# An attention and experts layer on one core: the gate is projected turned, head outputs are scaled by ScalarE after the last product and added by GpSimd

## The chip, the core and the metric

The kernel runs on one core of a Trainium2 chip. The metric is device time in microseconds (us) of one execution; lower is better. A core has TensorE (PE in the profile) for matmuls, VectorE (DVE), ScalarE (ACT) and GpSimd (POOL) for elementwise work, and the SP queue, which only issues DMAs here. TensorE writes to PSUM banks; GpSimd works in SBUF alone in this kernel.

## The reference

2048 tokens of width 256. 16 query heads and 4 key/value heads of 128; each group of 4 query heads shares a key/value head. Beside attention there are 8 experts, of which each token takes two. Cut to what matters:

```
xn = layernorm(x)
q, gate, k, v = split(xn @ w_qkv.T)
q, k = rope(layernorm(q)), rope(layernorm(k))
out  = softmax(causal(q @ k.T / sqrt(128))) @ v
out  = (out * sigmoid(gate)) @ w_o.T
x    = x + out + experts(xn)
```

## The kernel before

The outer loop runs over 4 groups g (one key/value head, 4 query heads), the inner one over 16 tiles t of 128 tokens. A tile (g, t) has t + 1 blocks of keys, so tiles grow towards the end of a group. A step of a tile has a name, and each engine has one queue in which the steps stand in an order written out by hand as a string of letters (`ORDERS`; `QUEUES` says which letter stands for which kind). Between engines, steps wait on semaphores alone. `BANKS` gives each step of TensorE that fills a PSUM bank one of five banks; `FREED_BY` names the step that lets it go. Two more banks hold turned scores (`pt_bank`), one holds the head outputs (`o_bank`).

f32 products are made of three passes (`three`, L1270): each operand is split into a high part, rounded to fp32r by ScalarE (`..._hi`), and the rest, by VectorE (`..._lo`). A turn is a transpose by TensorE.

The steps of a tile, by engine:

- `Q`, `KV`, `G` (TensorE, L1316): projections, tokens on the partitions. `G` fills one bank of 512 columns for the 4 heads: six passes.
- `q_take`, `kv_take` (ScalarE), `sumsq`, `same`, `rope_b` (VectorE), `swap`, `rstd` (GpSimd): layernorm and rope. `QT`, `KT` (TensorE) turn the result, `q_hi`, `q_lo` and so on split it.
- `scores` (TensorE), `max` (VectorE), `exp` (ScalarE, with row sums), `turn_probs` (TensorE), `p_hi`, `p_lo`, then `pv` (TensorE, L1358): the head outputs, with the head's dimension on the partitions and tokens on the columns, two heads (a half p) at a time, into `o_bank`.
- `inv` (VectorE, L1204): one over the row sums, `row_inv`.
- `tanh` (ScalarE, L873): sigmoid is (1 + tanh(gate / 2)) / 2; the half is in `w_o`. `gate_scale` (L905): four pieces of 128 columns, (tanh + 1) * `row_inv`, where tokens lie on the partitions, so that the row's scale is one number a partition. `GT` (TensorE, L1366): four turns bring the gate to the layout of the head outputs.
- `o_take` (ScalarE, L923): `o_bank` to `oT`, half by half; `pv` of the next tile waits for it. `og` (VectorE, L1210): `oT` times the turned gate. `og_hi` (L933), `og_lo` (L1215): its split.
- `OUT` (TensorE, L1374): 12 passes of 256 columns, summed over the 4 heads in one bank. `out_add` (VectorE, L1223): that bank is added to `acc`.

At the start `x` comes in five parts; `stats`, `x_rstd`, `norm` normalise a part (`xn`, L999), `XT`, `xT_hi`, `xT_lo` (L1004) turn and split it. `L`, `LT`, `route` choose the experts. The experts' steps (`XS`, `H`, `Y`, `fc_lo` ...) are strewn among the rest; GpSimd writes their rows with `scatter` and `y_place`. At the end `comb` (L1254) adds them to `acc`, and six stores write it out.

## Time and profile before

| | |
|---|---|
| median of 3 executions | 1523.54 us (1523.23 to 1524.11) |
| the profiled execution | 1523.42 us, of which the span from first to last instruction 1521.5 us |
| TensorE busy, matmuls | 1493.0 us, 98% of the span |
| VectorE, ScalarE, GpSimd busy | 1302.6, 1157.4, 369.3 us |
| granted clock of TensorE | 0.997 of 2.4 GHz |

Busy times are unions of an engine's instructions. A matmul's duration goes from its start to the end of its results, so neighbours overlap; what one more costs is the distance between starts.

### The profile page before, as it was taken

What the parts mean: (1) busy time and instruction counts of PE and PEld (TensorE: products, weight loads), DVE (VectorE), ACT (ScalarE), POOL (GpSimd) and SP (SyncE); (2) the same over time, 40 slices, a digit from 0 to 9 for tenths busy, and PEclk for the clock granted to TensorE, in tenths of its full rate; (3) what the DMA queues carried; (4) which work ended last, traced back from release to release, by engine and by line L of the source; (5) the groups of instructions that cost most, each with busy time, mean ns of one, the idle gap of its engine ahead of it and who ended that gap; (6) DMA issues with size and microseconds to landing.
All of it is one profiled execution on the core that took longest, in us unless ns stands there. A gap on an engine that the chain in (4) does not pass through costs nothing.

```text
span 1521.5 us, 29718 instructions
## 1 busy us (share of the span) xinstructions
PE 1493.0 (98%) x10589; PEld 1378.2 (91%) x10589; DVE 1302.6 (86%) x3037; ACT 1157.4 (76%) x3017; POOL 369.3 (24%) x502
## 2 busy tenths in 40 slices
PE   4999999999999999999999999999999999999998
PEld 3889999999999999999999999999999999999998
DVE  8999888888998888778799898877879988897888
ACT  3777777778888778777888777777788877767775
POOL 6644443330332211111032221111103231011010
PEclk9999999999999999999999999999999999999999
DMA  5510111002221021111122010111022111001014
GB/s 167 168 58 33 43 36 34 29 29 76 68 60 49 9 70 39 35 43 39 56 74 77 22 49 12 49 29 39 8 88 74 60 50 32 29 22 32 9 50 125
DMA packets 45124, 78.82 MB, mean 52 GB/s; under 512 B 4784, under 2 KB 30896, under 8 KB 44784
## 3 DMA queue, kind: packets, MB, share of 16 engines
q1 hardware_dynamic: 41232, 66.65, 14.3%
q0 software_dynamic: 3744, 10.26, 1.9%
q8 instruction: 84, 1.38, 0.4%
q14 instruction: 64, 0.52, 0.1%
HBM read 58.25 MB, written 24.72 MB: 55 GB/s over the span
## 4 chain that ended last, share of the span: by engine, by line
PE 83%; DVE 9%; issue 3%; ACT 3%; DMA 1%; POOL 0%; SPq 0%; DVEq 0%; ACTq 0%; POOLq 0%
PE bank L1270 43%; PE o_bank L1270 22%; PE pt_bank L1345 14%; DVE pT_lo L1194 2%; PE bank L1323 2%; PE bank L1366 1%; DVE neg_chunk_max L1180 1%; DVE bank L1177 1%; ACT probs L895 1%; DVE t_same L1144 1%; PE bank L1387 1%; ACT pT_hi L914 1%; DVE t_same L1140 0%; ACT gate L905 0%; DVE sumsq L1112 0%
## 5 line engine op out<-in xcount | busy, mean ns | idle before, releaser
L895 ACT ACTIVATE probs<-bank,neg_max 128x512 f32<-128x512 f32 (+3 forms) x640 | 397.0, 629 | 91.5 <-DVE neg_max L1187 51.3
L1194 DVE TENSOR_TENSOR pT_lo<-pt_bank,pT_hi 128x512 fp32r<-128x512 f32 (+1 forms) x576 | 368.6, 654 | 91.4 <-ACT pT_hi L914 88.4
L914 ACT ACTIVATE pT_hi<-pt_bank 128x512 fp32r<-128x512 f32 (+1 forms) x576 | 324.5, 578 | 136.5 <-PE pt_bank L1345 98.4
L1270 PE MATMUL o_bank<-pT_hi,v_hi 128*128 128x256 f32 x1088 | 328.3, 302 | 0.8 <-DVE pT_lo L1194 0.4
L1345 PE MATMUL pt_bank<-ident_rows,probs 128*128 128x128 f32 x2176 | 310.8, 273 | 0.7 <-DVE pT_lo L1194 0.2
L1270 PE MATMUL o_bank<-pT_hi,v_lo 128*128 128x256 f32 x1088 | 307.2, 282 | 0.0
L1270 PE MATMUL o_bank<-pT_lo,v_hi 128*128 128x256 f32 x1088 | 306.5, 282 | 0.0
L1180 DVE TENSOR_REDUCE neg_chunk_max<-bank 128x1 f32<-128x512 f32 (+1 forms) x384 | 242.7, 649 | 41.5 <-PE bank L1270 40.6
L1345 PEld LDWEIGHTS pt_bank<-ident_rows,probs 128*128 128x128 f32 x2176 | 252.5, 140 | 21.7 <-DVE pT_lo L1194 2.9
L1270 PE MATMUL bank<-kT_hi,qT_hi 128*128 128x512 f32 (+3 forms) x640 | 243.0, 380 | 0.2 <-ACT probs L895 0.2
L1270 PE MATMUL bank<-kT_lo,qT_hi 128*128 128x512 f32 (+3 forms) x640 | 231.1, 361 | 0.0
L1270 PE MATMUL bank<-kT_hi,qT_lo 128*128 128x512 f32 (+3 forms) x640 | 231.1, 361 | 0.0
L1270 PEld LDWEIGHTS o_bank<-pT_hi,v_hi 128*128 128x128 f32 x1088 | 206.4, 190 | 6.5 <-DVE pT_lo L1194 2.6
L1270 PEld LDWEIGHTS o_bank<-pT_lo,v_hi 128*128 128x128 f32 x1088 | 206.9, 190 | 3.1
L1270 PEld LDWEIGHTS o_bank<-pT_hi,v_lo 128*128 128x128 f32 x1088 | 206.1, 189 | 0.0
L756 POOL TENSOR_TENSOR t_swap<-qk_raw,made_tables 128x256 f32<-128x256 f32 (+1 forms) x160 | 86.8, 574 | 416.4 <-ACT t_same L864 416.1
L1270 PE MATMUL bank<-w_hi,xT_hi 128*128 128x512 f32 (+1 forms) x384 | 145.7, 379 | 8.7 <-DVE w_lo L1102 8.5
L1270 PE MATMUL bank<-w_hi,xT_lo 128*128 128x512 f32 (+1 forms) x384 | 137.4, 358 | 0.0
L1270 PE MATMUL bank<-w_lo,xT_hi 128*128 128x512 f32 (+1 forms) x384 | 137.3, 358 | 0.0
L1270 PEld LDWEIGHTS bank<-kT_hi,qT_lo 128*128 128x128 f32 x640 | 120.4, 188 | 17.2
L1270 PEld LDWEIGHTS bank<-kT_hi,qT_hi 128*128 128x128 f32 x640 | 121.1, 189 | 14.8 <-ACT probs L895 2.7
L895 ACT ACTIVATION_READ_ACCUMULATOR probs<-bank,neg_max 128x1 f32 x640 | 134.1, 210 | 0.0
(167 smaller groups left out, 2856.1 us busy)
## 6 DMA issues: line engine op xcount, KB each, us to landing
norm_rows<-kept_tables SPq DMA_DIRECT2D x24, 384.0 KB, 3.2
made_tables<-kept_tables SPq DMA_DIRECT2D x24, 384.0 KB, 3.3
kept_tables<-made_tables SPq DMA_DIRECT2D x16, 384.0 KB, 2.5
rows<-xs SPq DMA_DIRECT2D x23, 258.0 KB, 2.7
expert_raw<-in_w_fc SPq DMA_DIRECT2D x23, 256.0 KB, 3.1
expert_raw<-in_w_proj SPq DMA_DIRECT2D x23, 256.0 KB, 2.8
xs<-in_x_fill SPq DMA_DIRECT2D x11, 516.0 KB, 5.7
w_raw<-in_w_in SPq DMA_DIRECT2D x7, 640.0 KB, 4.3
```

The lines of the kernel that those rows point to most:

```text
L756: ins = pool.tensor_tensor(t_swap[:, heads, to], qk_raw[:, heads, of], rotary(g, t)[:, 1, i:i + 1, to].to_broadcast([P, count, 64]), ALU.mult)
L895: act.activation(probs[:, u, h % 2, first:first + width], bank("scores", g, t, h, c)[:, 0:width], ACT.Exp, bias=neg_max[:, u, h % 2:h % 2 ...
L914: act.activation(pT_hi[:, n % PT_RING, 0:width], pt_bank[n % 2][:, 0:width], ACT.Copy)\
L1144: ins = dve.scalar_tensor_tensor(rotated[:, h, :], t_same[:, h, :], rstd[:, h:h + 1], rotary(g, t)[:, 2, h // HG, :], ALU.mult, ALU.add)
L1177: ins = dve.tensor_tensor_reduce(scores, scores, mask[:, CHUNK - width:CHUNK], 1.0, least, ALU.add, ALU.min, to)
L1180: ins = dve.tensor_reduce(to, scores, AX.X, ALU.min)
L1194: dve.tensor_tensor(pT_lo[:, n % PT_RING, 0:width], pt_bank[n % 2][:, 0:width], pT_hi[:, n % PT_RING, 0:width].bitcast(F32), ALU.subtract) ...
L1270: ins = pe.matmul(out_ap, s, m, start=(start and done == 1), stop=(stop and done == last))
L1323: ins = pe.transpose(bank("QT", g, t)[:, h * P:(h + 1) * P], rotated[:, h, :], ident_f[:])
L1345: ins = pe.transpose(pt_bank[n % 2][:, (2 * jj + hh) * P:(2 * jj + hh + 1) * P], probs[:, p, hh, j * P:(j + 1) * P], ident_f[:])
L1366: ins = pe.transpose(bank("GT", g, t)[:, h * P:(h + 1) * P], gate[:, t % 2, h * D:(h + 1) * D], ident_f[:])
L1387: ins = pe.transpose(bank("XS", m)[:, (2 * c + k) * P:(2 * c + k + 1) * P], rows[:, k, c * P:(c + 1) * P], ident_f[:])
```

## The change

- `G` is projected turned: the weights of one head are the stationary operand and 256 tokens (two tiles, a pair) the moving one. A step `G` (g, pair, head) makes six passes of 256 columns. `tanh` writes it to `gateT` for each head. `GT` and `gate_scale` are gone.
- `og0` (VectorE) makes (tanh + 1) times `o_bank` in one instruction, half by half, straight from the bank to `oT`; `o_take` and `og` are gone. The row sums aren't in it yet. `og_hi` and `og_lo` form all four heads at once as before (the last tile in halves, as before).
- `OUT` no longer sums the heads: each half p fills a bank with the product of its two heads side by side. `o_scale` (ScalarE) multiplies each by its column of `row_inv`, one into `oT` (which is free by then), one into `o_rows` (in the place of `ogT_lo`). `out_add` (GpSimd) adds both to `acc`, one after the other. Only the last tile's is left to VectorE (`out_last`).
- `row_inv` has two buffers. `comb` and the stores wait for GpSimd's additions too. The orders of all engines and the banks are written anew.

```diff
--- before.py
+++ after.py
-FREED_BY = {"Q": "q_take", "KV": "v_lo", "G": "tanh", "QT": "q_lo", "KT": "k_lo", "GT": "og", "OUT": "out_add",
+FREED_BY = {"Q": "q_take", "KV": "v_lo", "G": "tanh", "QT": "q_lo", "KT": "k_lo", "OUT": "o_scale",
...
-    "dve": ("BCGHDHGGBGBBCCBJKDDJJCDDALLDDCPPKJPPJEQJQDEMDLLEIPPKJPPJMJNEQQLLOFPFFPPKPJJQQJNMNQLOLQFFPKPJJPPJMQNQNFLL"
+    "dve": ("BCGHDGBGCGHDDABBBCKCJDJEJDDDLLCOOOKJJEOPJMEDNPLLDINOOKJJOOJEFFFNPLLPKJOOOFMJFFNJNOPPFFFFLNMLPKJOPOOJNJPN"
...
-            add('pe G', ('G', g, t))
+            if t % 2 == 0:
+                for h in range(HG):
+                    add('pe G', ('G', g, t // 2, h))
+                    add('act gate', ('tanh', g, t // 2, h))
...
-            add('act gate', ('tanh', g, t))
             add('dve gate', ('inv', g, t))
-            add('act gate', ('gate_scale', g, t))
-            if (g, t) == LAST_TILE:
-                add('pe GT', ('GT', g, t))
-                for p in range(HG // 2):
-                    add('dve out', ('og', g, t, p))
+            for p in range(HG // 2):
+                add('dve og', ('og0', g, t, p))
+            for p in range(HG // 2):
+                if (g, t) == LAST_TILE:
                     add('act og', ('og_hi', g, t, p))
                     add('dve og', ('og_lo', g, t, p))
-                add('pe OUT', ('OUT', g, t))
-                add('pe OUT', ('OUT_rest',))
-                add('dve out', ('out_add', g, t))
-            else:
-                add('pe GT', ('GT', g, t))
-                add('dve out', ('og', g, t))
-                add('act og', ('og_hi', g, t))
-                add('dve og', ('og_lo', g, t))
-                add('pe OUT', ('OUT', g, t))
-                add('dve out', ('out_add', g, t))
+                elif p:
+                    add('act og', ('og_hi', g, t))
+                    add('dve og', ('og_lo', g, t))
+            for p in range(HG // 2):
+                add('pe OUT', ('OUT', g, t, p))
+                if (g, t) == LAST_TILE:
+                    add('dve out', ('out_last', g, t, p))
+                else:
+                    add('act out', ('o_scale', g, t, p))
+                    add('pool out', ('out_add', g, t, p))
...
-                add('act O', ('o_take', g, t, p))
...
-        gate = sb("gate", [P, 2, QW])
+        gateT = sb("gateT", [P, HG, 2 * P])
...
+        with nc.sbuf_tensor("o_rows", [P, HG // 2, C], F32) as o_rows:
+            pass
...
-            "GT": lambda g, t: (og_done, g * T + t + 1),
-            "OUT": lambda g, t: (acc_done, acc_number["out_add", g, t]),
+            "OUT": lambda g, t, p: (o_scaled, number["o_scale", g, t, p]),
...
+                elif kind == "out_add":
+                    g, t, p = a
+                    n = number[step]
+                    w.wait_ge(o_scaled, number["o_scale", g, t, p])
+                    if n > 1:
+                        w.wait_ge(pool_added, n - 1)
+                    pool.tensor_tensor(acc[:, t, :], acc[:, t, :], oT[:, 256 * p:256 * p + 256], ALU.add).then_inc(pool_step, 1)
+                    w.wait_ge(pool_step, n)
+                    pool.tensor_tensor(acc[:, t, :], acc[:, t, :], o_rows[:, p], ALU.add).then_inc(pool_added, 1)
...
-                    g, t = a
-                    n = g * T + t
-                    w.wait_ge(filled, fill["G", g, t])
-                    if n >= 2:
-                        w.wait_ge(filled, fill["GT", *tile_before(g, t, 2)])
-                    act.activation(gate[:, t % 2, :], bank("G", g, t)[:], ACT.Tanh, scale=0.5).then_inc(gate_done, 1)
+                    g, q, h = a
+                    n = g * T + 2 * q
+                    w.wait_ge(filled, fill["G", g, q, h])
+                    if n:
+                        w.wait_ge(o_gated, 2 * (n - 1) + h // 2 + 1)
+                    act.activation(gateT[:, h], bank("G", g, q, h)[:, 0:2 * P], ACT.Tanh, scale=0.5).then_inc(gate_done, 1)
...
-                elif kind == "gate_scale":
-                    g, t = a
+                elif kind == "o_scale":
+                    g, t, p = a
                     n = g * T + t
+                    w.wait_ge(filled, fill["OUT", g, t, p])
                     w.wait_ge(inv_done, n + 1)
-                    w.wait_ge(gate_done, n + 1)
-                    for h in range(HG):
-                        gh, inv = gate[:, t % 2, h * D:(h + 1) * D], row_inv[:, h:h + 1]
-                        ins = act.activation(gh, gh, ACT.Identity, bias=inv, scale=inv)
-                    ins.then_inc(gated, 1)
+                    for i, rows_to in enumerate((oT[:, 256 * p:256 * p + 256], o_rows[:, p])):
+                        h = 2 * p + i
+                        ins = act.activation(rows_to, bank("OUT", g, t, p)[:, i * C:(i + 1) * C], ACT.Copy,
+                                             scale=row_inv[:, t % 2, h:h + 1])
+                    ins.then_inc(o_scaled, 1)
...
-                elif kind == "o_take":
-                    g, t, p = a
-                    n = g * T + t
-                    w.wait_ge(pv_done, number["pv", g, t, p, (t + 2) // 2 - 1])
-                    if n:
-                        w.wait_ge(og_lo_done, n)
-                    act.activation(oT[:, 256 * p:256 * p + 256], o_bank[:, 256 * p:256 * p + 256], ACT.Copy)\
-                        .then_inc(o_copied, 1)
                 elif kind == "og_hi":
-                    g, t, p = a if len(a) == 3 else (*a, None)
-                    n = g * T + t
-                    cols = slice(0, QW) if p is None else slice(256 * p, 256 * p + 256)
-                    if n:
-                        w.wait_ge(filled, fill["OUT", *tile_before(g, t)])
-                    w.wait_ge(og_done, n + 1 + (p or 0))
+                    g, t = a[0:2]
+                    p = a[2] if (g, t) == LAST_TILE else 1
+                    cols = slice(256 * p, 256 * p + 256) if (g, t) == LAST_TILE else slice(0, QW)
+                    w.wait_ge(o_gated, 2 * (g * T + t) + p + 1)
                     act.activation(ogT_hi[:, cols], oT[:, cols], ACT.Copy).then_inc(og_hi_done, 1)
...
-                elif kind == "og":
-                    g, t, p = a if len(a) == 3 else (*a, None)
-                    cols = slice(0, QW) if p is None else slice(256 * p, 256 * p + 256)
-                    w.wait_ge(filled, fill["GT", g, t])
-                    w.wait_ge(o_copied, 2 * (g * T + t) + (2 if p is None else p + 1))
-                    dve.tensor_tensor(oT[:, cols], bank("GT", g, t)[:, cols], oT[:, cols], ALU.mult).then_inc(og_done, 1)
+                    if i >= 2:
+                        w.wait_ge(o_scaled, number["o_scale", *tile_before(g, t, 2), 1])
+                    dve.reciprocal(row_inv[:, t % 2], row_sum[:]).then_inc(inv_done, 1)
+                elif kind == "og0":
+                    g, t, p = a
+                    n, q = g * T + t, t // 2
+                    cols, tokens = slice(256 * p, 256 * p + 256), slice((t % 2) * P, (t % 2 + 1) * P)
+                    w.wait_ge(pv_done, number["pv", g, t, p, (t + 2) // 2 - 1])
+                    w.wait_ge(gate_done, number["tanh", g, q, 2 * p + 1])
+                    if n:
+                        w.wait_ge(pool_added, number["out_add", *tile_before(g, t), p])
+                    dve.scalar_tensor_tensor(oT[:, cols].rearrange("p (h q) -> p h q", h=2), gateT[:, 2 * p:2 * p + 2, tokens], 1.0,
+                                             o_bank[:, cols].rearrange("p (h q) -> p h q", h=2), ALU.add, ALU.mult).then_inc(o_gated, 1)
                 elif kind == "og_lo":
-                    g, t, p = a if len(a) == 3 else (*a, None)
-                    cols = slice(0, QW) if p is None else slice(256 * p, 256 * p + 256)
-                    w.wait_ge(og_hi_done, g * T + t + 1 + (p or 0))
+                    g, t = a[0:2]
+                    cols = slice(256 * a[2], 256 * a[2] + 256) if (g, t) == LAST_TILE else slice(0, QW)
+                    w.wait_ge(og_hi_done, number["og_hi", *a])
                     dve.tensor_tensor(ogT_lo[:, cols], oT[:, cols], ogT_hi[:, cols].bitcast(F32), ALU.subtract)\
                         .then_inc(og_lo_done, 1)
-                elif kind == "out_add":
-                    g, t = a
-                    w.wait_ge(filled, fill["OUT", g, t])
-                    if (g, t) == LAST_TILE:
-                        w.wait_ge(last_out, 1)
+                elif kind == "out_last":
+                    g, t, p = a
+                    w.wait_ge(filled, fill["OUT", g, t, p])
+                    w.wait_ge(inv_done, g * T + t + 1)
+                    w.wait_ge(pool_added, number["out_add", g - 1, t, 1])
                     w.wait_ge(acc_done, acc_before[step])
-                    dve.tensor_tensor(acc[:, t, :], bank("OUT", g, t)[:, 0:C], acc[:, t, :], ALU.add)\
-                        .then_inc(acc_done, 1)
+                    for i in range(2):
+                        h = 2 * p + i
+                        dve.scalar_tensor_tensor(acc[:, t, :], bank("OUT", g, t, p)[:, i * C:(i + 1) * C], row_inv[:, t % 2, h:h + 1],
+                                                 acc[:, t, :], ALU.mult, ALU.add).then_inc(acc_done, 1)
+                        w.wait_ge(acc_done, acc_number[step] - 1 + i)
...
+                    w.wait_ge(pool_added, number["out_add", G - 2 if t >= LATE_COMB else G - 1, t, 1])
...
+                elif kind == "G":
+                    g, q, h = a
+                    tokens = slice(2 * q * P, 2 * (q + 1) * P)
+                    cols = slice(QW + 2 * D + h * D, QW + 2 * D + (h + 1) * D)
+                    w.wait_ge(wg_lo_done, 2 * g + 2)
+                    w.wait_ge(xT_lo_done, 2 * part_of(2 * q + 1) + 1)
+                    three(bank("G", g, q, h)[:, 0:2 * P], [(w_hi[:, c, cols], w_lo[:, c, cols]) for c in range(CT)],
+                          [(xT_hi[:, c, tokens], xT_lo[:, c, tokens]) for c in range(CT)]).then_inc(filled, 1)
...
-                        w.wait_ge(o_copied, 2 * (g * T + t) + p)
+                        w.wait_ge(o_gated, 2 * (g * T + t) + p)
...
-                elif kind == "GT":
-                    g, t = a
-                    w.wait_ge(gated, g * T + t + 1)
-                    for h in range(HG):
-                        ins = pe.transpose(bank("GT", g, t)[:, h * P:(h + 1) * P],
-                                           gate[:, t % 2, h * D:(h + 1) * D], ident_f[:])
+                elif kind == "OUT":
+                    g, t, p = a
+                    w.wait_ge(og_lo_done, number["og_lo", g, t, p] if (g, t) == LAST_TILE else number["og_lo", g, t])
+                    w.wait_ge(wo_lo_done, g + 1)
+                    for i in range(2):
+                        h = 2 * p + i
+                        rows_of = slice(h * P, (h + 1) * P)
+                        ins = three(bank("OUT", g, t, p)[:, i * C:(i + 1) * C], [(ogT_hi[:, rows_of], ogT_lo[:, rows_of])],
+                                    [(wo_hi[:, h, :], wo_lo[:, h, :])])
                     ins.then_inc(filled, 1)
-                elif kind == "OUT":
-                    g, t = a
-                    w.wait_ge(og_lo_done, g * T + t + 1)
-                    w.wait_ge(wo_lo_done, g + 1)
-                    heads = range(HG) if (g, t) != LAST_TILE else range(HG // 2)
-                    three(bank("OUT", g, t)[:, 0:C], [(ogT_hi[:, h * P:(h + 1) * P], ogT_lo[:, h * P:(h + 1) * P]) for h in heads],
-                          [(wo_hi[:, h, :], wo_lo[:, h, :]) for h in heads], stop=(g, t) != LAST_TILE).then_inc(filled, 1)
-                elif kind == "OUT_rest":
-                    g, t = LAST_TILE
-                    w.wait_ge(og_lo_done, g * T + t + 2)
-                    heads = range(HG // 2, HG)
-                    three(bank("OUT", g, t)[:, 0:C], [(ogT_hi[:, h * P:(h + 1) * P], ogT_lo[:, h * P:(h + 1) * P]) for h in heads],
-                          [(wo_hi[:, h, :], wo_lo[:, h, :]) for h in heads], start=False).then_inc(last_out, 1)
```

## Rows read from the trace of the kernel before

**Rows 1.** The page: busy times, and the engines' shares of the chain that ended last.

```profile
PE 1493.0 (98%) x10589; PEld 1378.2 (91%) x10589; DVE 1302.6 (86%) x3037; ACT 1157.4 (76%) x3017; POOL 369.3 (24%) x502
...
PE 83%; DVE 9%; issue 3%; ACT 3%; DMA 1%; POOL 0%; SPq 0%; DVEq 0%; ACTq 0%; POOLq 0%
```

**Rows 2.** Three stretches: length, busy of PE, PEld, DVE, ACT, POOL, clock, DMA.

```profile
0.00:60.00 60.00, 38.88 (x223) 30.82 (x223) 51.80 (x149) 32.90 (x88) 38.98 (x60) 0.94 0.52 172
60.00:1480.00 1420.00, 1416.62 (x10086) 1312.73 (x10086) 1214.18 (x2814) 1100.47 (x2875) 330.29 (x443) 1.00 0.15 45
1480.00:1521.50 41.50, 37.49 (x283) 34.68 (x281) 36.63 (x76) 24.04 (x56) 0.00 (x0) 0.98 0.37 115
```

**Rows 3.** The table of waits, TensorE: what for, us in total, times, longest.

```profile
PE bank L1270 <- DVE w_lo L1102: 8.5, 1, 8.5
PE bank L1284 <- DVE xn L999: 5.8, 2, 5.2
PE bank L1323 <- DVE t_same L1144: 4.2, 2, 3.3
PE bank L1284 <- DVE v_lo L1133: 3.5, 2, 3.3
```

**Rows 4.** The chain of waits, 1495 us to the end: start, length, what.

```profile
1496.61 1.39 PE bank L1270 x6
1498.00 0.44 PE pt_bank L1345 x4
1498.44 0.73 PE o_bank L1270 x6
```

**Rows 5.** The chain of waits, 1508 us to the end.

```profile
1515.98 0.39 ACT oT L923
...
1517.38 0.44 DVE ogT_lo L1215
...
1517.86 0.99 PE bank L1270 x6
...
1518.97 0.42 DVE acc L1223
```

**Rows 6.** TensorE's groups of instructions, shapes apart.

```profile
L1366 PE MATMUL bank<-ident_rows,gate 128*128 128x128 f32 x256 | 38.4, 272 | 0.0
```

**Rows 7.** ScalarE's groups of instructions, shapes apart.

```profile
L905 ACT ACTIVATE gate<-gate,row_inv 128x128 f32<-128x128 f32 x256 | 105.6, 492 | 3.8 <-DVE row_inv L1204 2.8
...
L895 ACT ACTIVATE probs<-bank,neg_max 128x256 f32<-128x256 f32 x112 | 53.9, 483 | 6.2 <-DVE neg_max L1177 6.1
L923 ACT ACTIVATE oT<-o_bank 128x256 f32<-128x256 f32 x128 | 50.0, 391 | 22.5 <-PE o_bank L1270 19.8 <-DVE ogT_lo L1215 2.4
L933 ACT ACTIVATE ogT_hi<-oT 128x512 fp32r<-128x512 f32 x63 | 40.0, 635 | 16.2 <-DVE oT L1210 16.0
...
L873 ACT ACTIVATE gate<-bank 128x512 f32<-128x512 f32 x64 | 38.3, 598 | 8.9 <-PE bank L1270 8.6
```

**Rows 8.** VectorE's groups of instructions, shapes apart.

```profile
L1210 DVE TENSOR_TENSOR oT<-bank,oT 128x512 f32<-128x512 f32 x63 | 43.0, 683 | 3.8 <-PE bank L1366 3.6
```

**Rows 9.** Lines by themselves: count, shortest, median and longest in ns.

```profile
L1223 DVE TENSOR_TENSOR acc<-bank,acc x64: 394/415/426, 65.2 to 1519.0; 128x256 f32<-128x256 f32 x64
...
L1254 DVE SCALAR_TENSOR_TENSOR acc<-y_rows,p,acc x32: 472/484/486, 1474.5 to 1518.2; 128x256 f32<-128x256 f32 x32
...
L745 POOL TENSOR_TENSOR made_tables<-made_tables,t_swap x16: 729/738/1803, 20.3 to 306.7; 128x256 f32<-128x256 f32 x16
...
L1215 DVE TENSOR_TENSOR ogT_lo<-oT,ogT_hi x65: 412/682/1257, 56.2 to 1517.4; 128x512 fp32r<-128x512 f32 x63, 128x256 fp32r<-128x256 f32 x2
```

**Rows 10.** The timeline's start, VectorE and TensorE.

```profile
17.34 4.53 DVE L999 TENSOR_SCALAR xn<-acc,probs 128x256 f32<-128x256 f32 x7
...
24.48 1.01 DVE L1004 TENSOR_TENSOR xT_lo<-bank,xT_hi 128x384 fp32r<-128x384 f32 x2
...
28.81 1.09 PE L1323 MATMUL bank<-ident_rows,t_same 128*128 128x128 f32 x4 [3.29 <-DVE t_same L1144]
```

202 lines of the change are left out of this document (103 added, 99 removed).

## The prediction, made before the changed kernel was run

> **What bounds the kernel now.** I read the page's busy times first: TensorE is busy 98% of a span of 1521.5 us, VectorE 86%, ScalarE 76%, GpSimd 24% [rows 1]. A busy matmul row is a modelled time, so I asked next where TensorE stands still. The stretches answer that: in 0 to 60 us it idles 21.1 us, in 60 to 1480 us only 3.4 of 1420, in the last 41.5 us 4.0 [rows 2]. The table of TensorE's waits says that 22.0 us of it are four waits of the start: for a split weight, for xn, for the rotated heads, for a bank [rows 3]. So from 60 us on TensorE's own instructions set the time, nearly one for one, and the other engines matter only where they come to hold it up. In the chain of waits near the end the pieces of TensorE follow each other without a gap, and give prices by difference of starts: four f32 turns of 128 columns 0.44 us, six passes of 256 columns 0.72 us, six passes of 512 columns 1.39 us [rows 4]. These are the prices to use; the mean of one turn, 272 ns [rows 6], is latency and overlaps its neighbours.
>
> **TensorE's part of the change.** Removed: `GT`, 64 steps of four turns [rows 6]: 64 x 0.44 = 28.2 us. Changed: `G`. Before, 64 steps of six passes of 512 columns: 64 x 1.39 = 89.0 us. After, for each pair of tiles and each head six passes of 256 columns: 32 x 4 x 0.72 = 92.2 us, so 3.2 us more. `OUT` keeps its 12 passes of 256 columns a tile, in two banks instead of one: nothing, and `scores`, `turn_probs`, `pv`, `Q`, `KV` and the experts keep theirs. Sum: -28.2 + 3.2 = -25.0 us. Bounds: a turn has as many columns as half a pass of 256, so it can't well cost less than 0.06 us, which leaves a gain of 12 us; the 0.44 for four is measured between steps of `pv` and others, where `GT` stood too, so I hold to it. If the smaller passes cost exactly half of the large ones (64 x 1.39 for all), the gain is 28.
>
> **ScalarE's part.** Removed: 256 pieces of the gate's scaling 105.6 us, 128 copies of `o_bank` 50.0 us, 64 tanh of 512 columns 38.3 us [rows 7], together 193.9. Added: 128 tanh of 256 columns, at the price of the 256-column copy, 0.39 us: 50 us; and 252 `o_scale` pieces of 256 columns out of a bank, with a scale read from memory. No row shows that one. The copy without such an operand, 0.39 us, is below it; the exp of 256 columns, which reads one such operand, 0.48 us; the gate's scaling reads two and takes 105.6/256 = 0.41 us for 128 columns, so for 256 at most 0.52. I take 0.48: 121 us, with 98 to 131 as bounds. Net -23 us (-46 to -13): ScalarE is no nearer to being the bound.
>
> **VectorE's part.** Removed: 63 `og` of 512 columns 43.0 us and two of 256, 0.8; 63 `out_add` at 0.42, 26 us [rows 8]. Added: 128 `og0` of 256 columns (one scalar_tensor_tensor). The nearest rows are the 256-column addition out of a bank, 0.42, and the `comb` form, 0.48 [rows 8, 9]: 54 to 61 us, I take 0.45, 58 us; and `out_last`, 4 x 0.48 = 1.9 against one 0.42. Net about -11 us. Per microsecond of TensorE's work it stays as loaded as it was (1292 of 1468 against 1303 of 1493), and in 60 to 1480 it still has some 200 us of idle time [rows 2].
>
> **GpSimd's part.** 126 `out_add` steps, each two additions of 128x256 that depend on each other. The row for just this form, `made_tables`, has a median of 738 ns, at worst 1803 [rows 9]. 252 x 0.74 = 186 us: from 369 to 555 us, 36% of the span. This is hidden as work; it counts only as a delay.
>
> **The waits.** (a) *The head outputs.* `pv` of the next tile waited for `o_take`, now for `og0`, which waits for `tanh` and for GpSimd's `out_add` of the tile before, since `oT` is also where scaled rows go. In VectorE's queue, behind a waiting `og0`, stand `p_lo` and `max`, and TensorE waits for those. From an end of `OUT` (half 0) the way is two `o_scale` 0.96, two additions 1.5 to 1.6, then `og0` 0.45: 3.0 us, if GpSimd is free; a `swap`, `rstd` or `y_place` ahead adds 1 to 2. I laid TensorE's step prices along the new order string: from the end of `OUT` (g, t, 0) to the first `pv` that needs `og0` of the next tile freed, there are 7.8 us or more for every tile. So TensorE's direct wait is covered with 4 us to spare. ScalarE's queue gets two waits of the kind too: `tanh` of the next pair waits for `og0` of the tile before (one buffer of `gateT` where `gate` had two), `o_scale` for `OUT`; behind them stand `exp` and `p_hi`. GpSimd's `out_add` waits for `o_scale`, and behind it stand `swap`, `rstd` and `y_place`, of which `QT` needs the first two, some 2 tiles ahead. All three are covered while `og0` is in time. (b) *`og_hi` and `og_lo`.* They now come after `og0` of half 1: 0.45 + 0.64 + 0.68 = 1.8 us to `OUT` [rows 7, 9]. The same count over the string gives 2.0 us or more between the last `pv` of a tile and `OUT`, but for one place: at tile (1, 0) only one `turn_probs` of 0.44 stands between. There I expect a wait of 1.4 us. (c) *Banks.* 64 more fills of `G`, 64 more of `OUT`, 64 fewer of `GT`: 64 more in all over the same five banks, but `OUT` is let go after 0.96 us. I cost it at nothing: 1239 fills instead of 1175 over five banks in 1500 us are one for each bank in 6.1 instead of 6.4 us, and most are held for a pass of TensorE and one or two short instructions. If that cover is gone, it is rival C. (d) *The start.* VectorE's new order puts `norm` 3, `xT_lo` 1 and 2 and `wr_lo` ahead of `sumsq` (0, 0). That is four norms (2.6 us by the 4.53 for seven, 1.7 at the 0.42 of another 256-column instruction), 1.0 us, and a short one for which I put 0.4: `QT` (0, 0) falls 3.1 to 4.0 us later than 28.8 [rows 9, 10]. But `L` 0 (six passes of 512 columns, 1.39), `LT` 0 (four small turns, 0.3) and an `XT` of 0.44 have moved into that gap. So +1.0 to +1.9; I take 1.5. (e) *The end.* After the last `pv`: before, `o_take` 0.39, `og`, `og_hi`, `og_lo` 0.44, `OUT` 0.99 and `out_add` 0.42, from 1515.98 to 1519.39 [rows 5]. After: no copy, but `og_lo` twice and two dependent `out_last` pieces of 0.48 for each half in place of one of 0.42: -0.4 + 0.4 + 0.5 = +0.5 us. The stores keep their form. SP's queue has as many steps as before.
>
> **The sum.** The profiled execution took 1523.4 us against a median of 1523.5, so nothing is to be corrected. 1523.4 - 25.0 + 1.5 + 1.4 + 0.5 = 1501.8 us.
>
> **Weighed against this: the shared port.** [Rows 9] show an `og_lo` of 1257 ns beside a median of 682, and a GpSimd addition of 1803 beside 738: either engine is now and then held about one instruction of the other. The Trainium skill, page "SBUF — State Buffer", section "SBUF: two separate sides", states an exclusive lock between a GpSimd operation and a VectorE one with two SBUF inputs, in which the loser fully blocks; the long durations agree with it. In rows: GpSimd's additions cover 186 of 1502 us, 12%. About 620 VectorE instructions read two SBUF operands (`same`, `rope_b`, `og_lo`, the expert splits). 12% of them are 76, each held 0.37 on average: 28 us more on VectorE. Were each on TensorE's path, the time would be 1530; with VectorE's idle time as cover, I give half of it in the rival and nothing in the forecast.
>
> **Rivals.** *A, slower: the loop through GpSimd.* In 32 of the 63 tiles, by the count above, less than 3.0 us of TensorE's work lies between the end of `OUT` (half 0) and the end of the next tile's last `pv` of that half; there `og0` waits in VectorE's queue with `p_lo` behind it. For it: the chain that ended last lies for 9% of the span on VectorE and for 3% on ScalarE [rows 1], so in places TensorE already runs just behind them. Against it: the two banks and three buffers of turned scores that lie between, and that TensorE lost 3.4 us in 1420 with a queue like this. It decides from 22/32 = 0.7 us of TensorE's time for each such tile on; at 1.2 us the time is 1501.8 + 38 = 1540. *B, the shared port*, as above: 1501.8 + 14 = 1516, or 1508 at a quarter. *C, most of the gain goes into waits at banks and `og0`*, 0.35 us in each of the 63 tiles: 1501.8 + 22 = 1524, no change. For it: more hand-overs between engines; against: ScalarE and VectorE each have less to do. *D, more gain*: passes at half price, no stall at the start or at (1, 0): 1523.4 - 28 = 1495.5.
>
> **How the numbers follow.** Forecast (1497 to 1507) 0.58, B 0.16, D 0.10, C 0.06, A 0.10. About 0.2% (3 us) is what a measurement can tell from no change. Faster: forecast, B and D, 0.84. Same: C, 0.06. Slower: A, 0.10. Leaving out A, C and the edges of B and D gives 1494 to 1514.
>
> **What would show it.** Right: TensorE's busy time near 1468, no wait of TensorE over 2 us after 60 us but near tile (1, 0), GpSimd near 555 us, `o_scale` 0.45 to 0.52, idle time of 60 to 1480 under 8 us. Wrong: TensorE's idle time between 60 and 1480 us above 15 us, with `p_lo` or `scores` as what ends it and `og0` waiting for GpSimd (A); `og_lo` and `rope_b` clearly longer in the mean (B); busy time of TensorE fallen by less than 20 us (the price of a turn).

## The result: 1.1% slower, where 1.4% faster was forecast

| | before | after | forecast |
|---|---|---|---|
| median | 1523.8 us | 1541.2 us (1540.2 to 1541.9) | 1501.8, range 1494 to 1514 |
| ratio | | 1.0113, 95% interval 1.0102 to 1.0125 | 0.986 |
| span of the profiled execution | 1521.5 | 1540.0 | |

One of the four executions of the kernel before took 1631.4 us, over 7% above the other three, and the ratio leaves it out.

The page of the changed kernel, busy times and the engines' shares of the chain that ended last (before: [rows 1]):

```profile
PE 1487.3 (97%) x10717; PEld 1380.4 (90%) x10717; DVE 1321.8 (86%) x3040; ACT 1122.9 (73%) x2949; POOL 561.7 (36%) x754
...
PE 73%; DVE 13%; issue 7%; POOL 4%; ACT 2%; DMA 1%; SPq 0%; DVEq 0%; POOLq 0%; ACTq 0%
```

TensorE is busy 6 us less, not 25; VectorE is busy 19 us more, not 11 less; its share of the chain is 13% where it was 9%. GpSimd is near where it was expected (561.7 against 555). The three stretches (before: [rows 2]):

```profile
0.00:60.00 60.00, 38.43 (x202) 30.60 (x203) 49.87 (x140) 27.86 (x70) 35.68 (x59) 0.89 0.49 159
60.00:1480.00 1420.00, 1393.59 (x10110) 1298.58 (x10110) 1219.87 (x2795) 1058.54 (x2792) 519.80 (x687) 1.00 0.14 45
```

TensorE's idle time between 60 and 1480 us is 26.4 us where it was 3.4: the prediction had named 15 as the sign that it is wrong. The table of TensorE's waits (before: [rows 3]):

```profile
PE bank L1347 <- DVE t_same L1147: 15.4, 14, 2.5
PE bank L1300 <- DVE xn L1002: 13.6, 2, 8.4
PE bank L1313 <- ACT logit_rows L826: 3.0, 2, 2.3
PE pt_bank L1369 <- ACT probs L909: 2.7, 4, 0.9
PE bank L1286 <- DVE ogT_lo L1227: 2.7, 3, 1.3
PE pt_bank L1369 <- DVE pT_lo L1197: 2.6, 7, 0.8
```

At the top stands a wait that was 4.2 us in two places and is now 15.4 in 14: `QT` for `rope_b`. VectorE's and GpSimd's groups say why (out<-in, count, busy us, mean ns, idle before):

```profile
L1147 DVE SCALAR_TENSOR_TENSOR t_same<-t_same,rstd,made_tables 128x128 f32<-128x128 f32 x200 | 68.1, 406 | 1.5
L1143 DVE TENSOR_TENSOR t_same<-t_same,t_swap 128x640 f32<-128x640 f32 x64 | 56.5, 883 | 1.1
L1221 DVE SCALAR_TENSOR_TENSOR oT<-gateT,o_bank 128x256 f32<-128x256 f32 x128 | 52.9, 414 | 21.3 <-PE o_bank L1286 11.6 <-POOL acc L788 8.0 <-ACT gateT L887 1.0
L1227 DVE TENSOR_TENSOR ogT_lo<-oT,ogT_hi 128x512 fp32r<-128x512 f32 x63 | 46.0, 730 | 3.3 <-ACT ogT_hi L936 3.3
...
L1147 DVE SCALAR_TENSOR_TENSOR t_same<-t_same,rstd,norm_rows 128x128 f32<-128x128 f32 x120 | 43.1, 423 | 0.8
```

```profile
L788 POOL TENSOR_TENSOR acc<-acc,o_rows 128x256 f32<-128x256 f32 x126 | 101.0, 802 | 9.9
L786 POOL TENSOR_TENSOR acc<-acc,oT 128x256 f32<-128x256 f32 x126 | 95.2, 756 | 336.3 <-ACT o_rows L919 333.2
```

`rope_b` has not been changed, but its 128-column pieces last 406 and 423 ns in the mean. In the kernel before the same form stands at

```profile
L1144 DVE SCALAR_TENSOR_TENSOR t_same<-t_same,rstd,made_tables 128x128 f32<-128x128 f32 x200 | 56.1, 347 | 1.4
```

A place in the timeline of the changed kernel shows it at work (start, length; other rows between them left out):

```profile
1183.65 0.82 DVE L1143 TENSOR_TENSOR t_same<-t_same,t_swap 128x640 f32<-128x640 f32 x1
...
1184.06 0.28 PE L1286 MATMUL o_bank<-pT_lo,v_hi 128*128 128x256 f32 x1
...
1184.18 0.28 PE L1286 MATMUL o_bank<-pT_hi,v_lo 128*128 128x256 f32 x1
1184.20 0.85 POOL L786 TENSOR_TENSOR acc<-acc,oT 128x256 f32<-128x256 f32 x1 [0.74 <-ACT o_rows L919]
...
1184.51 2.28 DVE L1147 SCALAR_TENSOR_TENSOR t_same<-t_same,rstd,norm_rows 128x128 f32<-128x128 f32 x5
1185.13 0.72 POOL L788 TENSOR_TENSOR acc<-acc,o_rows 128x256 f32<-128x256 f32 x1
...
1186.94 1.08 PE L1347 MATMUL bank<-ident_rows,t_same 128*128 128x128 f32 x4 [2.48 <-DVE t_same L1147]
...
1187.89 0.77 PE L1286 MATMUL bank<-w_hi,xT_hi 128*128 128x512 f32 x1
```

The two additions fall on `rope_b`, its five pieces take 2.28 us, and TensorE stands for 2.48. The five pieces by themselves (shortest, median and longest in ns; then the first one alone):

```profile
L1147 DVE SCALAR_TENSOR_TENSOR t_same<-t_same,rstd,norm_rows x5: 337/339/875, 1184.5 to 1186.5; 128x128 f32<-128x128 f32 x5
...
1184.51 0.70 DVE L1147 SCALAR_TENSOR_TENSOR t_same<-t_same,rstd,norm_rows 128x128 f32<-128x128 f32 x1
```

Three of them are as short as ever; the two that meet an addition take 0.70 and 0.88 us, and end at 1185.20 and 1186.00, each 0.15 us after an addition has ended (1185.05 and 1185.85). So it is in the whole trace: of the 320 pieces 57 overlap an addition, in 24 of the 64 `rope_b`, and last 719 ns in the mean; the other 263 last 346. 42 of the 57 last over 500 ns, and every one of these ends 0.146 to 0.161 us after an addition. A piece isn't slowed by an addition, it stands until the addition is over. Why do they meet? In GpSimd's queue `out_add` often stands behind `rstd`, and `rope_b` comes some time after `rstd` too. It isn't `rstd` that starts it, though: here `rstd` was done at 1183.47, VectorE still had `same` to do, and over the whole run the first piece starts 2.4 us (median) after the end of its `rstd`. (The two passes above also show what the page's busy time hides: a row lasts 0.28 us, the next starts 0.12 us later. A wait of up to 0.16 us between two such passes leaves no gap in the busy time.)

### The profile page after: what moved, and what is told of

Same layout as the page of the kernel before. It is cut to its first block, busy times and chain, and to the rows that moved or that the text cites. A ratio compares the mean times of both kernels' runs of the same rounds, so it can differ in the third digit from the quotient of the medians.

```text
span 1540.0 us, 30508 instructions
## 1 busy us (share of the span) xinstructions
PE 1487.3 (97%) x10717; PEld 1380.4 (90%) x10717; DVE 1321.8 (86%) x3040; ACT 1122.9 (73%) x2949; POOL 561.7 (36%) x754
## 4 chain that ended last, share of the span: by engine, by line
PE 73%; DVE 13%; issue 7%; POOL 4%; ACT 2%; DMA 1%; SPq 0%; DVEq 0%; POOLq 0%; ACTq 0%
PE bank L1286 38%; PE o_bank L1286 20%; PE pt_bank L1369 12%; DVE t_same L1147 3%; PE bank L1347 2%; DVE pT_lo L1197 2%; POOL t_swap L761 1%; DVE neg_chunk_max L1183 1%; DVE bank L1180 1%; DVE t_same L1143 1%; POOL rstd L770 1%; DMA w_raw<-in_w_in 1%; DVE sumsq L1115 1%; POOL acc L788 1%; DVE t_same L1131 1%
## 5 line engine op out<-in xcount | busy, mean ns | idle before, releaser
L1369 PE MATMUL pt_bank<-ident_rows,probs 128*128 128x128 f32 x2176 | 316.6, 274 | 5.9 <-ACT probs L909 2.7
L786 POOL TENSOR_TENSOR acc<-acc,oT 128x256 f32<-128x256 f32 x126 | 95.2, 756 | 336.3 <-ACT o_rows L919 333.2
L795 POOL DMA_INDIRECT y_of<-rows,row_to x46 | 47.6, 1035 | 224.7 <-issue 184.8
L1286 PEld LDWEIGHTS bank<-kT_lo,qT_hi 128*128 128x128 f32 x640 | 121.7, 190 | 8.4
```

The source lines that it names most:

```text
L786: pool.tensor_tensor(acc[:, t, :], acc[:, t, :], oT[:, 256 * p:256 * p + 256], ALU.add).then_inc(pool_step, 1)
L795: pool.indirect_dma_start(y_of, bass.IndirectOffsetOnAxis(row_to[:, k:k + 1], 0), rows[:, k, 0:C], None)\
L1286: ins = pe.matmul(out_ap, s, m, start=(start and done == 1), stop=(stop and done == last))
L1369: ins = pe.transpose(pt_bank[n % 2][:, (2 * jj + hh) * P:(2 * jj + hh + 1) * P], probs[:, p, hh, j * P:(j + 1) * P], ident_f[:])
```

## The experiments

Eighteen runs, each beside the kernel before on the same chip. "After" stands for the changed kernel. Where a run is compared with one of another group, it is by the ratios.

**1. The additions, taken away or replaced.** Theory P: GpSimd's additions hold VectorE's instructions with two operands in SBUF. Theory Q: the way through GpSimd's queue is too long. Theory O: the new order of the steps costs the time, whatever GpSimd does.

```diff
-                    pool.tensor_tensor(acc[:, t, :], acc[:, t, :], oT[:, 256 * p:256 * p + 256], ALU.add).then_inc(pool_step, 1)
-                    w.wait_ge(pool_step, n)
-                    pool.tensor_tensor(acc[:, t, :], acc[:, t, :], o_rows[:, p], ALU.add).then_inc(pool_added, 1)
+                    # a_no_adds: nothing; og0 waits for o_scale instead
+                    # a_fills_for_adds: five chained memsets of 128x176, one of a column, the same waits
```

(The expectation speaks of six memsets; it was five of 176 columns and one of a single column.)

> The changed kernel with GpSimd's 252 additions left out (the attention part doesn't reach the sum; og0 waits for o_scale instead). Changed kernel 1541, before 1524. Theory P (the additions hold VectorE's two-operand instructions at the shared port): VectorE's busy time falls from 1322 to about 1292 and rope_b's pieces from 406-423 ns back to 347; the time falls by most of the 43 us that TensorE lost, to 1500 to 1510. Theory Q (the additions delay swap and rstd in GpSimd's queue, and with them QT): the same fall, so this run doesn't tell P from Q. Theory O (the new order of the steps itself, above all at the start of the run and at the small tiles of each group, costs the time whatever GpSimd does): stays at 1530 or above, idle time of TensorE in 60 to 1480 us stays near 25 us.

> The changed kernel, each pair of additions replaced by six memsets of a spare tile, which read nothing, with the same waits and about the same length (some 1.6 us a step; the attention part doesn't reach the sum). Theory P (shared port): most of the loss goes, 1505 to 1515, rope_b's pieces near 347 ns. Theory Q (queue of GpSimd and the wait of og0): stays within 5 us of 1541. Theory O: stays near 1541 too, but then a_no_adds does as well.

Measured: without additions 1523.1 us, ratio 0.9987 (0.9977 to 0.9997); with memsets 1520.3, 0.9969 (0.9956 to 0.9981). In the second GpSimd is busy 529.9 us (561.7 with additions, 365.0 with nothing), and `og0` waits for it 9.0 us, as before, yet its page and its table of TensorE's waits say:

```profile
PE 1476.2 (97%) x10717; PEld 1375.6 (91%) x10717; DVE 1291.4 (85%) x3040; ACT 1121.6 (74%) x2949; POOL 529.9 (35%) x1258
```

```profile
PE bank L1352 <- DVE t_same L1152: 4.1, 4, 1.7
```

VectorE is at the forecast 1292 us, and `rope_b`'s pieces are at 347 and 348 ns. So of the distance between 1541 and the forecast, 0.0144 of the time, 22 us, is what the additions do to VectorE (19 by the run without any), and GpSimd's queue costs nothing that can be seen: Q's 1541 is out. The other 18 us are not theirs. P's own times, 1500 to 1510 and 1505 to 1515, were missed for that reason, and so were O's 1530 or more: each theory had been given the whole loss. That the run without additions is slower than the one with memsets is in its trace in part: TensorE stands 3.7 us for `oT` at 293 us, and runs slower behind it (granted clock 0.66 from 290 to 300 us); the times of its ten executions lie between 1519.9 and 1525.0.

**2. The additions alone, in the kernel before.** Behind each `rstd` of groups 1 to 3, GpSimd works on 256 columns that are free there; nothing waits for it.

```diff
                     pool.tensor_tensor(rstd[:], variance[:], minus_half[:], ALU.pow).then_inc(rstd_done, 1)
+                    if g:
+                        # b_adds_held_in_before only: w.wait_ge(rotated_done, n + 1)
+                        for i in range(4):
+                            w.wait_ge(spare_step, 4 * (n - T) + i + 1)
+                            pool.tensor_tensor(spare_rows, spare_rows, spare_rows, ALU.add).then_inc(spare_step, 1)
+                            # b_one_operand: pool.tensor_scalar(spare_rows, spare_rows, 1.0, None, ALU.mult)
+                            # b_fills: ten memsets of 128x176 in the place of the four
```

> The kernel before with four dependent additions of 128x256 on a spare tile in GpSimd's queue behind each rstd of groups 1 to 3 (192 in all, 142 us of GpSimd; nothing waits for them but GpSimd's queue). Theory P: they meet rope_b head on; its pieces go to 450 ns or more, VectorE +25 us, the time +10 to +25 (1534 to 1549). Theory Q: swap of the next tile comes up to 3.1 us later only where it was within that of the rstd before; small, +0 to +8. Theory O: no change, 1524.

> The same as b_adds_in_before with ten memsets of a spare tile (about the same 3.2 us) in place of the four additions. Theory P: no change, 1524 to 1527. Theory Q: the same time as b_adds_in_before. Theory O: no change.

> The kernel before with the same 192 extra dependent GpSimd additions of 128x256 as in the run that took 1562.8 us, but each four wait until VectorE has finished the rope_b of their own tile. Theory P: an addition that meets no rope_b costs little; rope_b's pieces at 350 ns, TensorE's waits for QT near 4 us, and 1524 to 1534. Rival P2 (each addition costs VectorE the same wherever it falls): 1550 to 1565.

> The kernel before with, in the place of the 192 extra additions (two reads of memory each), 192 multiplications of 128x256 by a constant, which read one operand. Theory P by reading as such: any instruction of GpSimd that reads memory holds VectorE's two-operand instructions for its length; so the loss goes with GpSimd's added busy time: if one takes 0.4 to 0.5 us instead of 0.74, the loss is 20 to 26 us, 1544 to 1550. Rival P3 (only instructions with two reads hold VectorE): 1520 to 1526, as with memsets. Rival P4 (one that reads a single operand holds it all the same and takes as long): near 1563.

| | ratio | to before | rope_b's pieces, two forms | VectorE busy (before 1302.6) | GpSimd's added work |
|---|---|---|---|---|---|
| 192 additions behind rstd | 1.0252 (1.0235 to 1.0269) | +37.8 us | 408, 495 ns | 1344.4 us | 141 us, 736 ns each |
| the same, held until rope_b is done | 1.0052 (1.0035 to 1.0069) | +7.9 | 348, 348 | 1311.8 | 122 us, 634 ns |
| 192 multiplications with one operand | 1.0040 (1.0026 to 1.0054) | +5.9 | 357, 369 | 1311.5 | 177 us, 921 ns |
| 480 memsets | 0.9984 (0.9975 to 0.9994) | -2.6 | 347, 347 | 1302.7 | 117 us, 245 ns |

(The first form, with `made_tables`, also counts the 80 pieces of group 0, where nothing was added; the second stands in groups 1 to 3 alone.)

GpSimd's groups in the held and the one-operand run:

```profile
L774 POOL TENSOR_TENSOR angles<-angles 128x256 f32<-128x256 f32 x192 | 121.7, 634 | 190.7 <-DVE t_same L1153 179.4
```

```profile
L773 POOL TENSOR_SCALAR angles<-angles 128x256 f32<-128x256 f32 x192 | 176.9, 921 | 12.0
```

Additions that nobody needs cost 38 us, and 30 of them go when only their moment changes. So theory P holds: what counts is which instructions of VectorE they meet, and `rope_b` is the dear one. The rival by which each addition costs the same wherever it falls is out (it had said 1550 to 1565). P's size was wrong: it had expected 25 us on VectorE and 10 to 25 in the time, and got 42 and 38. In the trace 87 pieces of `rope_b` meet an addition and last 697 ns, the other 233 last 345. And it isn't reading as such: 177 us of one-operand work at the same place cost 6, where P by reading had said 20 to 26. There 185 pieces meet a multiplication and last 373 ns, at most 495. The time grows by 0.9 of what VectorE's busy time grows by, with the additions held as without; of the 38 us 14 are waits of `QT` that the table shows (18.0 us against 4.2). That the rest comes by `QT` too is not shown. The 2.6 us that the memsets seem to gain are unexplained.

**3. Can the changed kernel be mended so?** Hold each addition until `rope_b` of the tile ahead is done (where VectorE doesn't need it first); or give the first scaled pieces memory of their own in groups 1 to 3, so that not `og0` but only the later `og_lo` waits for GpSimd; or both.

```diff
+                    # held: the last rstd ahead of this step in GpSimd's queue
+                    w.wait_ge(rotated_done, len(ropes))
                     if n > 1:
                         w.wait_ge(pool_added, n - 1)
+                    # apart: angles and norm_rows[:, 3] in the place of oT; og_lo, not og0, waits for pool_added
```

> The changed kernel, complete; in 110 of the 126 out_add steps GpSimd now waits, ahead of its first addition, until VectorE has finished the rope_b whose rstd stands last before it in GpSimd's queue (in the other 16 VectorE needs the addition first). The additions read as much memory as before and keep their place in every queue; they only no longer meet rope_b. Theory P (the additions hold VectorE's rope instructions, QT comes late): rope_b's 128-column pieces fall from 406 ns to near 350, TensorE's waits for QT from 15.4 us in 14 to 4 to 8 us, and the time from 1541 to 1525 to 1532; not to the 1520 of the fills, since the additions now meet og_lo and the splits instead. Rival P2 (what is held is VectorE's work in all, wherever the additions fall): pieces of rope_b at 350, but other two-operand lines longer by as much, and 1537 to 1543. Rival Q2 (a later addition holds og0, and what stands behind it): 1545 or more, with TensorE waiting for oT or pT_lo.

> The changed kernel, complete, but in groups 1 to 3 o_scale puts its first piece of each half into memory of its own (256 columns that held the angles, 256 that held a norm row) instead of oT. So og0 of the next tile no longer waits for GpSimd's additions; og_lo does, over a microsecond later, since it writes where the second pieces lie. The additions keep their number and place. Theory P alone (the additions cost by the instructions of VectorE that they meet, the way through GpSimd costs little while nothing is held): 1538 to 1542, rope_b's pieces still 400 to 410 ns. Rival A of the prediction (the way through GpSimd is itself dear): 1525 to 1533.

> The kernel of the run before (first pieces in memory of their own), complete, with each addition also held until rope_b of the tile ahead is done, where VectorE doesn't need it earlier. If holding the additions failed before only because og0 waited for them (33.7 us of VectorE's time), the two together give what each alone could not: rope_b's pieces near 350 ns, VectorE's wait of og0 for GpSimd under 5 us, and 1520 to 1527, near the run with fills. Rival (the port takes its toll from og_lo, same and the splits just as well): 1532 to 1542.

Measured: held 1.0130 (1.0113 to 1.0147), apart 1.0122 (1.0105 to 1.0138), both 1.0071 (1.0055 to 1.0088). After itself: 1.0113. The held run, `og0`'s group on VectorE:

```profile
L1226 DVE SCALAR_TENSOR_TENSOR oT<-gateT,o_bank 128x256 f32<-128x256 f32 x128 | 53.3, 416 | 45.7 <-POOL acc L793 33.7 <-PE o_bank L1291 10.1 <-ACT gateT L892 1.0
```

`rope_b` is back at 348 ns and VectorE at 1298 us, but `og0` now waits 33.7 us for GpSimd instead of 8.0, with `p_lo` and `max` behind it: the loss has moved, not gone. That is between rival P2's 1537 to 1543 and Q2's 1545 or more, and TensorE's 5.4 us of waits for `oT` are Q2's sign; P's 1525 to 1532 is missed. So the change has tied the additions from both sides. Early they meet `rope_b`, late they hold `og0`. With memory apart the second tie is loosened, and the two together give back 6 us that neither gives alone (apart alone: as the theory had it, with `rope_b` at 405 and 424 ns). My 1520 to 1527 was still too good, and the rival's 1532 to 1542 has the time, though not the mechanism: `og_lo` takes 721 ns there and 730 in after, `same` 727 and 740: `rope_b` was as short as expected (347 ns), but TensorE stood 4.6 us at one place near 515 us, where ScalarE and VectorE both waited for loads (an expert's weights, a rotation table); why these came late there was not followed up. It ends 10.7 us above before.

**4. The rest of the distance: start and gate.** Theory O: the new order of the start. VectorE does `rope_b` (0, 0) ahead of norm 3 and route 0, ScalarE the copy of logits 3 ahead of two exps, TensorE `QT`, `KT` (0, 0), `Q` (0, 1) ahead of `XT` 5 and 6 (first try; the second, shown below, leaves xT_lo 3 ahead of `same` (0, 0) and does xT_lo 4 too ahead of norm 3, since they free the banks).

```diff
+MOVES = (    # engine, step, the step that it now stands ahead of
+    ('dve', ('norm', 3), ('xT_lo', 5)),
+    ('dve', ('route', 0), ('xT_lo', 5)),
...
+    ('act', ('q_hi', 0, 0), ('xT_hi', 5)),
+    ('act', ('logit_copy', 3), ('exp', 0, 1, 2, 0)),
+    ('pe', ('QT', 0, 0), ('XT', 5)),
+    ('pe', ('KT', 0, 0), ('XT', 5)),
+    ('pe', ('Q', 0, 1), ('XT', 5)),
+)
```

> The changed kernel, complete, with a few steps of its first 55 us in another order: VectorE does the first tile's same and rope_b before norm 3, xT_lo 3 and route 0, q_lo and k_lo before xT_lo 5; ScalarE does q_hi and k_hi before xT_hi 5 and logit_copy 3 before two exps; TensorE does QT, KT and Q (0, 1) before XT 5 and 6. Banks stay with their steps. Theory O (a part of the loss is the new order of the start, with the slower clock that its idle time brings): QT (0, 0) at 27.5 to 28.5 us instead of 30.7, no wait of 2.4 us for logit_rows, and 4 to 6 us less in all: 1535 to 1537. Rival O2 (what is gained at the start is lost again, because the same chain of rope, exp and turned scores sets the pace of the first tiles): less than 1.5 us, 1540 to 1541.

> The changed kernel, complete, with the start in another order, mended after the first try, in which KT (0, 0) waited for a bank that xT_lo 4 frees: VectorE does rope_b (0, 0), xT_lo 3 and 4 before norm 3, route 0 and q_lo, k_lo; the rest as in the first try. Theory O: QT (0, 0) at 28 to 28.5 us, KT within 1.5 us behind it, no wait for logit_rows above 1 us, and 3 to 5 us less than 1541. Rival O2 (the first tiles' chain of rope, max, exp and turned scores sets the pace, and TensorE has too little other work until tile (0, 3)): 1539.5 to 1542.

> The changed kernel with tanh writing gateT as before but og0 reading a constant in its place, so that tanh, which has one buffer for a pair of tiles, no longer waits for og0 of the pair before (10.2 us of ScalarE's waits, in 6). The gate is left out of the result. If the single buffer of the gate is part of the loss (ScalarE stands still with exp and p_hi behind): 2 to 6 us less, 1535 to 1539, above all in the small tiles. If those waits are covered: 1540 to 1542.

Measured: 1.0146 (1.0129 to 1.0163), 1.0141 (1.0124 to 1.0158), gate 1.0131 (1.0114 to 1.0147). All three miss their times. In the first try `QT` (0, 0) starts at 28.9 instead of 30.7 us, but `KT` waits 2.3 us for its bank; in the second xT_lo 3 stands waiting in VectorE's queue with `same` behind it, and `QT` starts at 30.2. Neither order is a fair test of a better start; they show only that it isn't mended by moving a step or two. Without the wait for the single buffer of the gate nothing is gained (two executions took 1543.9 us, two 1547.3): ScalarE's 10.2 us of waiting there are covered.

**5. What is TensorE's work worth?** The prediction rests on the step that it is worth its length. Theory R: in the small tiles of each group VectorE is as full as TensorE, so that what TensorE is spared there turns into waiting. So: take work from TensorE alone, in the old order (one turn of the gate for four, 63 times; `og` multiplies all heads by that one in an instruction of the same size), from VectorE alone (`same` of one query head for four), and from ScalarE (one piece of the gate's scaling for four).

```diff
-                    for h in range(HG):
+                    for h in range(HG if (g, t) == LAST_TILE else 1):
                         ins = pe.transpose(bank("GT", g, t)[:, h * P:(h + 1) * P],
...
-                    dve.tensor_tensor(t_same[:, 0:HG, :], qk_raw[:, 0:HG, :],
+                    dve.tensor_tensor(t_same[:, 0:heads, :], qk_raw[:, 0:heads, :],
```

> The kernel before, its order unchanged, with one turn of the gate instead of four in 63 of its 64 GT steps; og multiplies all four heads by that one turned head, in one instruction of the same size, so VectorE's, ScalarE's and GpSimd's work stays. The other three heads' gates are left out of the result. Removed: 63 x 3 turns, 20.8 us of TensorE by the 0.44 for four. If TensorE's work is worth its length wherever it lies, as the prediction took it: 1502 to 1505. Theory R (in the small tiles of each group VectorE is as full as TensorE, 28 to 29 us of 30, so what TensorE is spared there turns into waiting): a gain of 12 to 16 us only, 1508 to 1512, with new waits of TensorE in the first eight tiles of the groups. Rival R2 (order and hand-overs bind everywhere): under 8 us of gain.

> The same shortening of same in the kernel before, for comparison: 27 us less of VectorE, TensorE's work unchanged, the same part left out of the result. TensorE waits 3.4 us there in 60 to 1480 us, so there is little to win: 1520 to 1523 by either theory. More than 5 us of gain would say that VectorE held TensorE back already, out of sight of the waits.

> The run with fills in the place of the additions, and in it the wide piece of same (VectorE, 0.70 us) multiplies one query head instead of four in 63 tiles: 0.42 us less of VectorE in each tile, 27 us in all, with no wait changed and TensorE's work unchanged. The rotation of three query heads is left out of the result. Theory R (VectorE's load in the small tiles holds back a part of TensorE's saving): 1512 to 1517 against 1520.3. Rival (what is left is the chain of hand-overs, or the start): 1519 to 1521.

> The kernel before with both cuts at once: one turn of the gate instead of four (20.8 us of TensorE, alone worth 6.7) and the short same (27 us of VectorE, alone worth 3.8); the same parts are left out of the result. If TensorE and VectorE bind together (each one's saving is held back by the other), the two give clearly more than their sum of 10.5: 15 to 22 us less, 1502 to 1509. If they are independent: 1512 to 1515. If a third thing binds (ScalarE, or the chain from one step to the next): 1512 to 1516 as well, and the next run tells.

> The kernel before with one turn of the gate instead of four and one piece of the gate's scaling on ScalarE instead of four in 63 tiles (77 us less of ScalarE, and the scaled gate 1.2 us earlier); only the first head's gate counts in the result. If ScalarE's queue is what holds TensorE's saving back: 1503 to 1511. If not: 1515 to 1518, as with the quarter turns alone.

> All three cuts in the kernel before: turns, same, and the gate's scaling. If all engines are tied to each other through the fixed order, this gives the 20.8 us of TensorE nearly whole: 1499 to 1504. If what holds the saving back is not the load of VectorE or ScalarE but the length of the chain for one block (scores, max, exp, turns, splits, pv), then no more than the run with the turns and same together.

| | taken away | ratio | to before |
|---|---|---|---|
| turns | TensorE 20.8 us by price | 0.9955 (0.9938 to 0.9972) | -6.7 us |
| same | VectorE 25 by its rows, 19 of busy time | 0.9975 (0.9964 to 0.9985) | -3.9 |
| turns and same | both | 0.9939 (0.9923 to 0.9956) | -9.3 |
| turns and gate's scaling | TensorE 20.8, ScalarE 64 of busy time | 0.9935 (0.9918 to 0.9951) | -10.0 |
| all three | all | 0.9912 (0.9895 to 0.9928) | -13.4 |
| memsets for additions, in the new order (experiment 1) | | 0.9969 (0.9956 to 0.9981) | -4.7 |
| the same and short same | VectorE 25 by its rows, 22 of busy time | 0.9931 (0.9914 to 0.9948) | -10.8 |

(The expectations put the work taken away at 27 and 77 us.) Of 20.8 us taken from TensorE, 6.7 arrive (4.3 to 9.4 by the interval). That refutes the one-for-one step for this kernel in its old order; what an order written anew for the lighter work would give was not run. The page of that run still looks as before:

```profile
PE 1484.0 (98%) x10400; PEld 1358.8 (90%) x10400; DVE 1302.3 (86%) x3037; ACT 1154.9 (76%) x3017; POOL 366.5 (24%) x502
```

```profile
60.00:1480.00 1420.00, 1412.33 (x9946) 1297.78 (x9946) 1219.02 (x2826) 1101.50 (x2884) 329.30 (x443) 1.00 0.14 45
```

98% busy, 7.7 us idle from 60 to 1480: 4.3 more than before, where 14 are missing. The rest are the waits too short to be seen whole in the busy time. (The Trainium skill, page "Perfetto Trace Analysis", in the note at its head, calls matmul busy time a bad metric, since matmuls are pipelined, and names MFU, the share of peak arithmetic, and the busy share of weight loads instead. That matmul busy time is a bad metric agrees with these rows; the share of weight loads would not have helped: PEld is 91% before and 90% here. MFU was not worked out.) To see them I gave each of TensorE's steps its price by difference of starts ([rows 4]; a 512-column pass 0.23, a turn 0.11) and took the sum along the order from the time between the first and the last step ("fills" are the memsets of experiment 1):

| waits of TensorE over its steps' prices, us | in all | 0 to 100 | 100 to 400 | 400 to 500 | 500 to 800 | 800 to 900 | 900 to 1100 | 1100 to 1300 | later |
|---|---|---|---|---|---|---|---|---|---|
| before | 38.5 | 24.2 | 1.5 | 1.2 | 3.1 | 1.8 | 0.5 | 3.0 | 3.1 |
| turns taken away | 53.7 | 26.0 | 3.8 | 2.6 | 5.9 | 3.3 | 2.1 | 5.5 | 4.5 |
| after, with fills | 61.5 | 31.0 | 7.8 | 7.1 | 4.5 | 2.6 | 1.3 | 5.0 | 2.2 |
| after | 81.7 | 32.4 | 6.2 | 8.9 | 4.2 | 8.3 | 3.4 | 13.5 | 4.8 |

The sums hang on the prices: with slightly other ones (0.2317, 0.1198, 0.1747 and 0.1093 us for passes of 512, 256 and 384 columns and a turn) they are 36.5, 51.7, 58.8 and 79.1, so 2 to 3 us lower each, and their differences within 0.7 us of these. By either, TensorE's steps add up to some 25 us less after than before, as the forecast had it. So the work went as said, and the waits grew by 43.

*In the old order* with the turns taken away the new waits are spread over all stretches. They aren't tiny: from 60 us on, those of 0.1 to 0.8 us go from 59 to 106 places and from 10 to 20 us. Most of the new ones stand before `scores`, `pv` and `turn_probs`. Theory R had them in the small tiles; here 30 us of the kernel before with small tiles, and 30 with large ones:

```profile
800.00:830.00 30.00, 30.00 (x215) 27.62 (x214) 28.79 (x76) 25.12 (x69) 9.03 (x13) 1.00 0.29 96
...
640.00:670.00 30.00, 29.80 (x215) 27.51 (x214) 23.86 (x54) 21.87 (x57) 5.75 (x7) 1.00 0.17 50
```

But the new waits are in both kinds of tile, and the short `same` gives 3.9 us in the old order and 6 in the new one: theory R holds in part at most. Nor do the loads bind together: turns and same give 9.3, their sum is 10.6. With all three taken away 13.4 arrive, where the single gains add up to 13.9 (6.7, 3.9, and 3.3 for the scaling). So each engine's load counts a little and by itself, and TensorE's 20.8 us are not whole with any. The last expectation is missed on both sides: neither 20 us came nor only the 9.3 that the length of the way of a block through the engines (scores, max, exp, turns, splits, `pv`, in a fixed order with two or three buffers) would have left. That way may still be what holds back the rest; no run shortened it, and it is not shown.

*In the new order* it is another matter, and the table says where. From before to "fills" 23.0 us of waits are new, and 19.0 of them lie in the first 500 us: 6.8 up to 100, 6.3 up to 400 (3.1 of them one wait near 300 us), 5.9 up to 500. In the thousand us behind that only 4.0 are new. TensorE is idle 5.8 us between 500 and 1480 us there, where it was 1.8, but 11.6 between 60 and 500, where it was 1.6:

```profile
60.00:500.00 440.00, 428.38 (x3112) 397.37 (x3111) 375.72 (x899) 325.53 (x871) 211.36 (x459) 1.00 0.17 54
500.00:1480.00 980.00, 974.23 (x7143) 914.65 (x7141) 833.60 (x1936) 745.55 (x1956) 280.27 (x729) 1.00 0.14 43
```

Laid side by side at the same `pv` passes, the run with fills is 19.2 us behind before at 472 us, with as much TensorE work done (0.4 us more), and 2.3 us ahead at the end, with 24.9 us less: 21.5 of 25.3 us arrive. Without the additions, TensorE's saving comes nearly whole in the new order from there on; what ate it lies ahead of that.

## Why the prediction was wrong, step by step

- *"From 60 us on TensorE's own instructions set the time, nearly one for one."* This step failed. It was read from 3.4 us of idle time, but a row of TensorE outlasts the pitch of its neighbours, and short waits fill it out. In the old order the turns' run gives 0.32 us of time for one of TensorE's. By that, 25 us would be worth 8, and with the 3.4 us that the sum adds for start, (1, 0) and end the time 1518.7. The run with fills, by its ratio, is at 1518.7 too, but that is luck: its table of waits has another shape. The sum gave the new order 3.4 us of waits in all; 19.0 new ones came in the first 500 us, and only 4.0 behind that, where TensorE's saving arrives nearly whole. So of the 17 us between 1501.8 and the run with fills, 4 at most are this step as it is written, and the rest are terms of the waits that were put too low or at nothing: the start, the way to 400 us, the first tiles of group 1 up to 500. The table of waits names `probs`, `pT_lo`, `ogT_lo` and `v_lo` as what ends the longer ones between 60 and 500 us; which of the new order's choices makes them was not run.
- *The shared port, "nothing in the forecast".* This is the dearest step that failed: 22 us, more than the 17 by which the kernel is slower than before. Rival B had the mechanism, with 28 us on VectorE and half of them on the path. VectorE got 30 (1321.8 against 1291.4), 25 of them in `rope_b`. Wrong was the half: 22 of the 30 arrived, since the additions fall on `rope_b`, on the way to `QT`, and not evenly on all that VectorE does. B ended at 1516, since it stood on the rest of the sum too. With both steps put right the sum closes: 1501.8 + 17 + 22 = 1541. The Trainium skill, page "SBUF — State Buffer", section "SBUF: two separate sides", has the rule that I weighed and set at nothing: an exclusive lock between a GpSimd instruction that reads SBUF and a VectorE one with two SBUF inputs, in which the loser fully blocks. The additions agree, piece by piece (42 long pieces, each ending 0.15 us after an addition), and so do the memsets, which cost nothing. The one-operand multiplications, which read SBUF for 921 ns each, don't: the 185 pieces that meet them last 373 ns.
- *TensorE's part, -25.0.* Right: about -25 by prices. Its busy time fell by 5.7 only, since waits too short for a gap count as busy. So "busy time fallen by less than 20 us", named as the sign that the price of a turn is wrong, came although that price was right.
- *ScalarE's part.* Inside its bounds: 1122.9 us, -34 against a forecast of -23 within -46 to -13. The prices of its rows, `o_scale` at 0.48 and `tanh` at 0.39, were exact:

```profile
L919 ACT ACTIVATE o_rows<-bank,row_inv 128x256 f32<-128x256 f32 x126 | 60.7, 482 | 0.0
...
L887 ACT ACTIVATE gateT<-bank 128x256 f32<-128x256 f32 x128 | 48.3, 388 | 32.2 <-PE bank L1286 21.5 <-DVE oT L1221 10.2
```

- *VectorE's part, -11.* Right without the additions (1291.4 from 1302.6); `og0` takes 414 ns, not 450.
- *GpSimd's part, 555 us.* 561.7; an addition takes 756 to 802 ns, not 738.
- *(a) The head outputs.* Half right. `og0` waits 8.0 us for GpSimd in 8 places, TensorE waits for `oT` 0.2 us. But "covered with 4 us to spare" held only while the additions start at once: held for `rope_b`, they took 33.7 us of VectorE's time. *(b) (1, 0):* a wait of 1.5 us was expected as 1.4; but `OUT` comes late at other places too: by the prices its passes start 7 us late in all, where before it was 2, most of them under a microsecond. Around it, from 400 to 500 us, 7.7 us of waits are new.
- *(c) Banks, nothing.* TensorE's table has no wait for `o_scale`; right as far as it shows.
- *(d) The start, +1.5.* `QT` (0, 0) came 1.9 us later (30.7 for 28.8), inside the +1.0 to +1.9. What was missed lies behind it: TensorE stands 2.3 us for the copy of the logits at 53.6, and its clock, 0.94 of full speed in the first 60 us before, is 0.89. To 100 us the waits are 32.4 for 24.2, so +8.2 and not +1.5.
- *(e) The end, +0.5.* Right: from the end of the last `pv` to that of the last addition it takes 3.9 us (1534.01 to 1537.88) where it took 3.4. A part of the chain:

```profile
1534.01 0.42 DVE oT L1221
1534.43 0.35 DVE ogT_lo L1227
...
1534.82 0.99 PE bank L1286 x6
...
1535.84 0.49 DVE acc L1237
```

- *Rival A* (slower, 1540) has the measured time, but not by its mechanism: with the same way through GpSimd and memsets on it, the kernel is 0.3% faster than before. The time came from B's and from the waits of the first 500 us; that it is A's number is chance.
- *What I had named as signs of being wrong* did show it: over 15 us of idle time from 60 to 1480; `rope_b` longer in the mean (the sign of B; `og_lo`, named with it, only went from 703 to 730 ns, and is at 729 with memsets too); and `p_lo` as what ends TensorE's waits, the sign of A, only 2.6 us of them.
- *A reading of the rows.* The "four waits of the start" are four groups with seven waits, and a turn's price of 0.44 for four holds for one by itself too (below).

**Left open.** In six of the ten profiles of the new order TensorE stands some 3 us more near 300 us, while GpSimd issues a row of scatters and VectorE waits; the chain names an unknown queue there. The profile of after doesn't have it, the one with fills does, and no run was made for it. It makes comparisons of single versions of the new order uncertain by some 3 us: additions against memsets may be worth 3 us more than the 22, and apart and held together more than the 6. What the start can give in a good order wasn't found. No version here beats the kernel before with the whole computation in it; the nearest is 0.7% behind.

## What to carry to other kernels

Before putting a TensorE saving into a sum one for one, take a little of its work away and run that: at 98% busy it was worth a third here in the old order. The saving isn't lost for good by that: in the new order it came nearly whole after 500 us, and the price was paid ahead of it, so compare two orders stretch by stretch and at the same step. Price steps by the difference of their starts and compare the sum with the time; busy time can't show waits shorter than a row's overlap. Elementwise work moved to GpSimd is priced by what VectorE does at that moment: an addition with two operands in the queue where `rope_b` falls, a VectorE step with two operands on the way to TensorE, cost 0.2 us of the whole each, held until that step was done 0.04; but then look who waits for it.

## What the runs showed of the hardware

- A 128-column VectorE instruction with two operands in SBUF (347 ns) that meets a GpSimd addition with two operands stands until the addition is over: in the run with 192 additions 87 pieces met one, lasted 697 ns in the mean, and each ended 0.144 to 0.153 us after an addition's end. Beside 192 multiplications with one operand (921 ns each) 185 pieces lasted 373 ns, and beside 480 memsets (245 ns) all stayed at 347. The three runs cost 38, 6 and no us. The addition is held too: 634 ns in the mean where it meets no `rope_b`, 736 in the run where many do.
- ScalarE's pass over 256 columns of a bank takes 388 ns (`tanh`) or 391 (the copy, [rows 7]), with a scale read from memory 482.
- Behind a wait TensorE can run at its lower level, 1.2 GHz, for some microseconds. Behind the 2.48 us above, six 512-column passes take 2.47 us by their starts (1187.89 to 1190.36) instead of 1.39, and the 30 us around it, which hold another wait, of 2.21 us, show a granted clock of 0.89 (third column from the end): there the late `QT` costs its wait and 1.1 us more. It isn't so behind every wait: behind one of 2.42 us in the run with 192 additions (at 1189.8 us) and one of 3.07 in the run with fills (at 300.7) the clock stays at its upper level, 2.4 GHz, and six such passes take 1.48 us behind the former.

```profile
1180.00:1210.00 30.00, 25.22 (x158) 23.16 (x157) 27.55 (x67) 20.03 (x55) 15.55 (x23) 0.89 0.19 62
```

- One f32 turn alone (the run with the turns taken away) costs 0.11 us by difference of starts, a quarter of four: the 0.03 to the next step and 0.08 more on that step's first pass.
